# Cross-attention block on one core: softmax sums after the product with V, an x turn behind Q, score groups and loads of the start respread, quotient on GpSimd

## What is computed

```python
x = layer_norm(hidden_states, ln1_w, ln1_b)
q, k, v = x @ q_w + q_b, ctx @ k_w + k_b, ctx @ v_w + v_b        # 16 heads of 32
attn = softmax(where(mask, q @ k.T / sqrt(32), min))             # over 512 keys
hidden = (attn @ v) @ cproj_w + cproj_b + hidden_states
y = layer_norm(hidden, ln2_w, ln2_b)
out = hidden + gelu(y @ fc_w + fc_b) @ proj_w + proj_b
```

## Time and profile before

| | us |
|---|---|
| three runs | 835.57, 841.01, 841.81 (median 841.01) |
| the profiled execution | 834.41, its span 832.6 |
| start, to the first `s2` | 129.8 |
| the 64 steps, from the first `s2` to the first feed-forward matmul | 329.0 |
| from there to the end | 373.9 |
| busy: PE, PEld, DVE, POOL, ACT | 776.1, 526.5, 462.1, 331.6, 284.9 |
| mean granted TensorE clock | 0.975 of 2.4 GHz |

### The profile page before, as it was taken

One profiled execution on the slowest core, in us unless ns is written; L12 is line 12 of the kernel. 1 busy time (PEld: TensorE's weight loads), 2 busy tenths in 40 slices (PEclk: granted clock), 3 DMA queues, 4 the chain that ended last, 5 costly groups with the idle time before them and its releaser, 6 DMA issues.

```text
span 832.6 us, 10079 instructions
## 1 busy us (share of the span) xinstructions
PE 776.1 (93%) x3728; PEld 526.5 (63%) x3728; DVE 462.1 (55%) x967; ACT 284.9 (34%) x495; POOL 331.6 (40%) x202
## 2 busy tenths in 40 slices
PE   7899988898899888988978899999999999999998
PEld 5788753343354334543432588888888888888886
DVE  6865386867766788568785834633323333332222
ACT  4433415766645563556445201121112110111110
POOL 2734402967656676567645535632001110112000
PEclk9999997999999999999996999999999999999999
DMA  8388997666556655435513144304000400011001
GB/s 303 128 285 297 294 258 272 151 154 144 151 141 173 162 148 141 115 78 151 127 42 111 64 140 120 95 1 152 1 0 1 152 1 0 1 62 41 0 1 50
DMA packets 60016, 97.99 MB, mean 118 GB/s; under 512 B 6112, under 2 KB 14564, under 8 KB 59968
## 3 DMA queue, kind: packets, MB, share of 16 engines
q1 hardware_dynamic: 59824, 97.34, 39.4%
q10 hardware_dynamic: 144, 0.02, 0.0%
HBM read 72.03 MB, written 25.18 MB: 117 GB/s over the span
## 4 chain that ended last, share of the span: by engine, by line
PE 72%; DVE 15%; DMA 4%; ACT 3%; issue 3%; SPq 2%; POOL 1%; DVEq 0%; ACTq 0%; POOLq 0%
PE ps L485 18%; PE ps L486 18%; PE ps L487 18%; DVE ps L957 7%; PE ps L582 6%; PE ps L598 4%; PE ps L610 4%; PE ps L567 3%; ACT Pt L778 2%; DVE R L982 1%; DMA qs<-BIG 1%; DVE R L915 1%; DMA R<-in_k_w 1%; DVE BIG L1007 1%; DVE mx L957 1%
## 5 line engine op out<-in xcount | busy, mean ns | idle before, releaser
L957 DVE CUSTOM_DVE_ANT_0 ps<-ps,FU 128x512 f32<-128x512 f32 x256 | 169.1, 723 | 54.9 <-PE ps L567 54.7
L778 ACT ACTIVATE Pt<-ps 128x512 f32<-128x512 f32 x256 | 139.2, 597 | 139.4 <-PE ps L582 136.5
L1110 DVE CAST HR<-R 128x512 fp32r<-128x512 f32 x52 | 24.5, 470 | 183.4 <-ACT R L820 183.4
L1230 POOL TENSOR_TENSOR R<-Pt 128x1024 f32<-128x1024 f32 x30 | 73.0, 2451 | 120.8 <-PE ps L610 77.9
L582 PE MATMUL ps<-BIG 98*128 98x512 f32 x256 | 102.9, 464 | 7.9 <-ACT Pt L778 5.2
L820 ACT ACTIVATE R<-ps,cols 128x512 f32<-128x512 f32 x52 | 35.9, 690 | 205.4 <-PE ps L487 205.4
L582 PEld LDWEIGHTS ps<-BIG 98*128 98x128 f32 x256 | 45.3, 196 | 77.0 <-ACT Pt L778 38.3
L485 PE MATMUL ps<-BIG,HR 128*128 128x512 f32 x192 | 74.9, 390 | 2.7 <-DVE HR L1112 2.7
L485 PE MATMUL ps<-YT,BIG 128*128 128x512 f32 x192 | 75.8, 395 | 0.0
L487 PE MATMUL ps<-YT,BIG 128*128 128x512 f32 x192 | 74.8, 390 | 0.0
L486 PE MATMUL ps<-YT,BIG 128*128 128x512 f32 x192 | 74.8, 390 | 0.0
(11 more groups left out here) (129 smaller groups left out, 1405.5 us busy)
## 6 DMA issues: line engine op xcount, KB each, us to landing
BIG<-qs SPq DMA_DIRECT2D x48, 256.0 KB
BIG<-ks SPq DMA_DIRECT2D x48, 256.0 KB
ks<-BIG SPq DMA_DIRECT2D x32, 256.0 KB, 2.9
qs<-BIG SPq DMA_DIRECT2D x32, 256.0 KB, 6.8
R<-hd SPq DMA_DIRECT2D x28, 256.0 KB, 4.3
R<-in_x SPq DMA_DIRECT2D x16, 256.0 KB, 4.3
hd<-R SPq DMA_DIRECT2D x16, 256.0 KB, 2.2
RW<-in_fc_w SPq DMA_DIRECT2D x16, 256.0 KB, 2.8
```

Source lines behind the costliest of these rows:

```text
L778: eng.activation(Pt[:, r, j % 2, :], bank(PSUM[("s2", i, j)][0]), ACT.Exp, scale=SCALE).then_inc(S["a_ra"], 1)
L957: eng.tensor_tensor_reduce(out=scores, in0=scores, in1=FU[:, s // 4 % 2, :], scale=1.0, scalar=-3.4e38, op0=ALU.add, op1=ALU.max, accum_ou ...
L1230: eng.tensor_tensor(pair_sums(s)[kc // 2][:, 2 * hp:2 * hp + 2, :], Pt[:, (r - 2) % 6, :, :], Pt[:, r, :, :], ALU.add).then_inc(S["g_ac"], 1)
```

## The change

- On TensorE, `sums(s - 1)` stands behind `pv(i - 1)` instead of ahead of it.
- `x_turn(1)`, `x_affine(1)` and `x_high(1)` stand behind all four Q units of batch 0.
- `s1` groups 0 and 1 go to the last two Q units of batch 2, groups 2 to 4 to K of batch 3, group 5 behind the first Q unit of batch 3, ahead of which the first maxima are turned. DVE's maxima follow.
- SP issues the first mask and two leading parts in batch 1. In batch 3 it issues `store_max(0)`, then stack 1, then the eight Q stores, then leading part 2, context 1, stack 2, and only then the projection weight. Before, stacks 1 and 2 stood ahead of K's and Q's stores of batch 3, and context 1 behind the weight.
- The V units of batch 1 start at step 4 and take three steps each; the context splits go to earlier steps.
- `divide_c` goes from DVE to GpSimd, at the head of its step `kc == 3`.
- Layer norm 2 of batch 0 goes to steps 36 to 46. Slab 4 is rounded at step 61 instead of behind the loop, and its low part is made on GpSimd. The last batch's output projection goes one step later.

```diff
@@ plan
-            PARTS[8 + 2 * c] = ([(u, 0)], [(u, 1)], [])
-            PARTS[9 + 2 * c] = ([(u, 2)], [(u, 3)], [])
+            PARTS[4 + 3 * c] = ([(u, 0)], [(u, 1)], [])
+            PARTS[5 + 3 * c] = ([(u, 2)], [], [])
+            PARTS[6 + 3 * c] = ([(u, 3)], [], [])
...
-        SLABS = (50, 56, 57, 60)
+        SLABS = (50, 56, 57, 60, 61)
@@ SP
-                if b == 3:
-                    load_stack(1)
                 for g in range(4):
                     store_qk(b, g, 0)
                 if b == 2:
-                    load_mask(0)
-                    load_lead(0)
-                    load_lead(1)
                     load_stack(0)
...
                 if b == 3:
-                    load_stack(2)
+                    store_max(0)
+                    load_stack(1)
                 for g in range(4):
-                    if b == 3 and g == 2:
-                        store_max(0)
                     store_qk(b, g, 1)
...
+                if b == 1:
+                    load_mask(0)
+                    load_lead(0)
+                    load_lead(1)
             load_lead(2)
+            load_context(1)
+            load_stack(2)
             sp.wait_ge("g_xl", 16)
             eng.dma_start(R2[:, :, :], kp(c_w)).then_inc(S["d_wc"], 16)
@@ TensorE
-                    if b == 3:
-                        s1(g)
+                    if b == 3 and g < 3:
+                        s1(2 + g)
...
-                    if b == 3 and g == 1:
+                    if b == 3 and g == 0:
                         turn_maxima(0)
                     proj_T(b, g, 1)
-                    if b == 0 and g == 1:
-                        x_turn(1)
-                    if b == 3 and g < 2:
-                        s1(4 + g)
+                    if b == 2 and g >= 2:
+                        s1(g - 2)
+                    if b == 3 and g == 0:
+                        s1(5)
+                if b == 0:
+                    x_turn(1)
...
+                if i:
+                    pv(i - 1)
                 if kc == 1 and s:
                     sums(s - 1)
-                if i:
-                    pv(i - 1)
@@ ACT
                     if b == 3 and g == 2:
                         copy_maxima(0)
                     qk_high(b, g, 1)
-                    if b == 0 and g == 1:
-                        x_high(1)
+                if b == 0:
+                    x_high(1)
@@ DVE
-                if kc == 3 and s:
-                    divide_c(s - 1)
...
-                if 30 <= i < 34:
-                    dve.wait_ge(f"d_h{i - 30}", 16)
-                    statistics(HN, 0, 4, i - 30)
...
-                if i in (36, 38, 40, 42):
-                    norm(HN, 0, 4, (i - 36) // 2)
+                if 43 <= i < 47:
+                    norm(HN, 0, 4, i - 43)
@@ GpSimd
+            def divide_c(s):
+                pool.wait_ge("v_t2", s + 1)
+                pool.wait_ge("a_pv", s + 1)
+                if s:
+                    pool.wait_ge("g_al", s)
+                eng.tensor_tensor(R1[:, 3, :], R1[:, 0, :], R1[:, 2, :], ALU.mult).then_inc(S["g_at"], 1)
...
+                if kc == 3 and s:
+                    divide_c(s - 1)
                 if kc % 2:
                     for hp in range(2 if i < 54 else 1):
```

More of the change, by code:

```diff
@@ L422, in _ @@
                     store_max(TURNS[i])
-                if i % 16 == 0 and b < 3:
+                if i in (16, 32):
                     load_context(b + 1)
@@ L457, in _ @@
                         eng.dma_start(ov[4 * (b - 1) + c], R2[:, c, :]).then_inc(S[f"d_o{c}"], 16)
-                if 2 <= i < 6:
-                    c = i - 2
+                if 4 <= i < 8:
+                    c = i - 4
                     sp.wait_ge("v_cp", 12 + c + 1)
@@ L715, in _ @@
                     pj(i - 1)
-                if 2 <= i < 6:
-                    if i < 4:
+                if 3 <= i < 7:
+                    if i < 5:
                         pe.wait_ge("a_pv", NS)
@@ L720, in _ @@
                     else:
-                        pe.wait_ge("v_cp", 12 + i - 3)
-                    cproj(3, i - 2, bank(6 + i % 2)).then_inc(S["p_cp"], 1)
+                        pe.wait_ge("v_cp", 12 + i - 4)
+                    cproj(3, i - 3, bank(6 + i % 2)).then_inc(S["p_cp"], 1)
                 if i < NJ and b + 1 < B and 11 <= f < 15:
@@ L782, in split_out @@
                 ta = R1[:, 3, :]
-                act.wait_ge("v_at", s + 1)
+                act.wait_ge("g_at", s + 1)
                 eng.activation(ta, ta, ACT.Identity, bias=vec[:, 4, g:g + 1]).then_inc(S["a_ab"], 1)
@@ L792, in copy_pv @@
                 if s:
-                    act.wait_ge("v_at", s)
+                    act.wait_ge("g_at", s)
                 else:
@@ L816, in gelu @@
                 elif i in (12, 13):
-                    act.wait_ge("v_at", NS)
+                    act.wait_ge("g_at", NS)
                 else:
@@ L868, in _ @@
                     split_out(s - 2)
-                if b < 3 and i % 16 in (3, 4, 6, 7):
-                    context_high(b + 1, (3, 4, 6, 7).index(i % 16))
+                t = i if b == 0 else i % 16 - 2
+                if b < 3 and 1 <= t < 5:
+                    context_high(b + 1, t - 1)
                 if i in YT_STEPS:
@@ L1007, in split_slab @@
                     eng.tensor_copy(sl[2 * h], RW[:, n, 512 * h:512 * h + 512]).then_inc(S["v_sh"], 1)
-                    if 2 <= f < 5:
+                    if f in (2, 3):
                         dve.wait_ge("v_sh", 2 * f + h + 1)
@@ L1043, in _ @@
                     qk_low(b, g, 0)
-                    if b == 3:
+                    if b == 3 and g < 3:
                         for j in range(4):
-                            maximum(4 * g + j)
+                            maximum(8 + 4 * g + j)
                 if 0 < b < 3:
@@ L1050, in _ @@
                     qk_low(b, g, 1)
-                    if b == 0 and g == 1:
-                        x_affine(1)
-                    if b == 3 and g < 2:
+                    if b == 2 and g >= 2:
                         for j in range(4):
-                            maximum(16 + 4 * g + j)
+                            maximum(4 * (g - 2) + j)
+                    if b == 3 and g == 0:
+                        for j in range(4):
+                            maximum(20 + j)
+                if b == 0:
+                    x_affine(1)
             for i in range(NI):
@@ L1086, in _ @@
                                       ALU.subtract).then_inc(S["v_wc"], 1)
-                if 30 <= i < 34:
-                    dve.wait_ge(f"d_h{i - 30}", 16)
-                    statistics(HN, 0, 4, i - 30)
-                if i == 34:
+                if 36 <= i < 40:
+                    dve.wait_ge(f"d_h{i - 36}", 16)
+                    statistics(HN, 0, 4, i - 36)
+                if i == 40:
                     variances(0, 4)
-                if i in (36, 38, 40, 42):
-                    norm(HN, 0, 4, (i - 36) // 2)
+                if 43 <= i < 47:
+                    norm(HN, 0, 4, i - 43)
                 if i in SLABS:
                     split_slab(SLABS.index(i))
-            split_slab(4)
             split_slab(5)
@@ L1115, in _ @@
                     divide_b(NS - 1)
-                    divide_c(NS - 1)
                 if i >= 1 and f == 0:
@@ L1121, in _ @@
                         eng.tensor_tensor(R2[:, c, :], bank(c), R2[:, c, :], ALU.add).then_inc(S["v_o"], 1)
-                if 2 <= i < 6:
-                    c = i - 2
+                if 3 <= i < 7:
+                    c = i - 3
                     dve.wait_ge("p_cp", c + 1)
@@ L1235, in _ @@
                     out_low(s - 2)
-                if b < 3 and i % 16 in (4, 6, 8):
-                    for k in {4: (0, 1), 6: (2,), 8: (3,)}[i % 16]:
+                t = i if b == 0 else i % 16 - 2
+                if b < 3 and 2 <= t < 5:
+                    for k in ((0, 1), (2,), (3,))[t - 2]:
                         context_low(b + 1, k)
@@ L1245, in _ @@
                     eng.tensor_tensor(R2[:, c, :], R2[:, c, :], cbt[:, :], ALU.add).then_inc(S["g_xc"], 1)
-                if i == 34:
+                if i == 41:
                     root(0, 4)
-                if i in SLABS[:2]:
+                if i in SLABS and SLABS.index(i) not in (2, 3):
                     slab_low(SLABS.index(i))
-            slab_low(5)
             for i in range(NJ):
@@ L1255, in _ @@
                 if i == 0:
+                    divide_c(NS - 1)
                     out_low(NS - 1)
+                    slab_low(5)
                 if 1 <= i < 10:
```

15 lines of the change are left out of this document (5 added, 10 removed).

## The result

| | before | after |
|---|---|---|
| median of 20 runs each, us | 839.13 (835.56 to 844.15) | 843.53 (841.10 to 847.31) |
| ratio after / before | | 1.005, 95% interval 1.0031 to 1.0068 |
| profiled execution, span | 834.41, 832.6 | 841.98, 840.2 |
| mean granted TensorE clock | 0.975 | 0.959 |

The change makes the kernel slower by 0.5%. The forecast was 838 against 841, so 0.4% faster. The loss is small, but its interval leaves out 1. The measured median lies on the wrong side of no change, 7.2 us off (+4.4 instead of -2.8), though inside the range.

A forecast was written before the change was run, and what follows sets the result against it. TensorE bounds the feed-forward part, so only its idle time in start and loop could give; 11.9 - 3.7 - 8.6 - 6.2 + 3.3 + 0.5 = -2.8 us on 834.4 gave 831.6, median forecast 838, range 829 to 851.

The forecast's parts named there:

- The start: Start of the loop: first maxima come earlier, but the projection weight lands at 150.0, delaying step 2's exponentials: +11.9 us.
- M: In the start, the time the first maxima are ready, for which SP waits ahead of stack 1: forecast 119.9, before 122.99.
- the x turn: Second x turn behind batch 0's Q units: the wait moves to Q's third unit, until 40.9; +0.6 us, inside the start's 11.9.
- The promised sign: Profile after: step 2's exponentials wait over 10 us for the weight, ending near 150; under 5 would refute the start's term.
- V spread: Steps 4 to 15: V's units spread at one part per step, 55.8 us becoming 51.9; -3.7 us.
- sums: Sums behind the product with V: the product fills TensorE's wait for the first maximum; -8.6 us, bounds 0 and -11.
- DVE relieved: Steps 40 and 56: norms and quotient no longer stand ahead of maxima on DVE; -6.2 us, bounds 0 and -8.
- Rival 3: Sums' wait only renamed: the next group waits for `divide_a` everywhere, 8.6 us comes back, 847; chance 0.10.
- The quotient on GpSimd: Quotient ahead of GpSimd's pair sums: late only at step 51 (2.5) and step 15 (+0.8); +3.3 us, bounds 0 and +14.
- the sign I had set: Profile after: ACT's L784 waits for GpSimd in step 51 alone; in more than five slices, rival 2 holds.
- rival 2: GpSimd becomes the gate: the quotient reaches ACT 1.3 us late in every slice; +13.4 us, so 854; chance 0.12.
- The joint: Joint ahead of the feed-forward part: slab 4 leaves, but the wait moves to GpSimd; +0.5 us, bounds -3 and +4.

The follow-up runs named there:

- experiment 2: Changed kernel with ACT's four projection-weight copies and DVE's low parts at steps 5 to 8 instead of 1 to 4, loads as changed: 836.3 us, ratio 0.9963 to the kernel before.
- experiment 4: Changed kernel with stack 2 and projection weight loaded in the loop, weight copies and DVE's low parts at steps 7 to 10: 829.02 us, ratio 0.9877 to the kernel before.
- experiment 1: Kernel before with only the sums moved behind the product with V: 833.55 us, ratio 0.9931 to the kernel before.
- experiment 5: Kernel before with only the quotient moved from DVE to GpSimd: 838.23 us, ratio 0.9964 to the kernel before.
- experiment 6: Kernel before with sums behind the product with V and layer norm 2 moved to steps 36 to 46, quotient on DVE: 832.25 us, ratio 0.9899 to the kernel before.
- experiment 3: Changed kernel with the quotient back on DVE at its old place: 844.18 us, ratio 1.0057 to the kernel before.
- experiment 7: Changed kernel with slab 4 split behind the loop again, both halves on DVE: 841.68 us, ratio 1.0011 to the kernel before.
- experiment 10: Changed kernel with GpSimd's third bias add of each batch moved from step 14 to behind step 15's last pair sums: 839.54 us, ratio 1.0006 to the kernel before.
- experiment 11: Experiment 9's kernel plus the third bias add behind the last pair sums: 825.32 us, ratio 0.9815 to the kernel before.
- experiment 12: Experiment 11's kernel with slab 0's low halves behind step 51's last pair sums and SP's reload of that buffer at step 53: 820.98 us, ratio 0.9776 to the kernel before.
- experiment 8: Experiment 4's kernel with slab 4 put back behind the loop: 829.18 us, ratio 0.9857 to the kernel before.
- experiment 9: Experiment 4's kernel with the next batch's context loaded ahead of batch 3's K stores: 827.57 us, ratio 0.986 to the kernel before.

## Why the prediction was wrong

**The start: mechanism right, size 2.7 us short.** The chain from the copy of the maxima to the weight was right to 0.1 us: forecast 30.1, measured 122.18 to 152.37, so 30.2. What was late was M itself, 122.18 instead of 119.9. The waits of 3.0 us in batch 3 were there (0.79, 0.77 and 1.56). Mis-sized were the groups and the x turn. I had taken a group at 0.44 us, but a unit with a group ahead of it and no wait takes 3.41 us from eviction to eviction instead of 2.72, so 0.69; six times the difference is 1.5 us. ACT in the changed kernel:

```profile
102.18 0.69 ACT L761 ACTIVATE BIG<-ps,cols 128x512 fp32r<-128x512 f32 x1 [3.54 <-PE ps L487]
105.59 0.69 ACT L761 ACTIVATE BIG<-ps,cols 128x512 fp32r<-128x512 f32 x1 [2.72 <-PE ps L487]
```

The trace of before shows the same:

```profile
111.04 0.69 ACT L759 ACTIVATE BIG<-ps,cols 128x512 fp32r<-128x512 f32 x1 [7.12 <-PE ps L487]
114.43 0.69 ACT L759 ACTIVATE BIG<-ps,cols 128x512 fp32r<-128x512 f32 x1 [2.70 <-PE ps L487]
```

The turn cost 0.9 us (batch 2's third Q unit is evicted at 94.57 instead of 93.64), not 0.6. Together these are 1.8 of the 2.3 us by which M is late.

The first score came at 126.58, not at 124. Landings followed the order of issue again: the rule of the Trainium skill ("DMA: Bandwidth & Descriptors", section "Queues, rings and completion order") that completion is not first in, first out did not help the weight here. It was issued at 140.06, last but the mask, and landed last but the mask, after 12.3 us. The promised sign, a wait for the weight over 10 us, was seen (11.61), and experiments 2 and 4, which take that wait away, gained 7.2 and 14.5 us. Part of the 2.7 us is the execution compared with: step 4 begins at 146.48 in the trace of before, but at 149.47, 152.64 and 148.08 in those of experiments 1, 5 and 6, whose start is the same; with the changed start it begins at 161.04, and at 161.35, 164.31 and 162.27 in experiments 3, 7 and 10. The middles of the two groups lie 13.0 us apart.

**V spread, sums, DVE relieved: right.** -3.7 against -3.7; steps 18 to 49 and 53 to 58 together -16.2 against -14.2. No wait of L610 for a maximum is left, step 40 takes 4.92 us (forecast 5.3), step 56 5.78. By experiment 6 it is the norms' move that mends step 40, and the quotient's that mends step 56. Rival 3 falls with experiment 1. But the measured 5.6 us (bounds 0 and -11) is below my 8.6, and not because the wait was renamed at its place: the steps without products gave 0.33 instead of 0.55, and steps 12 and 59 became longer by it.

**The x turn: right in the mechanism.** The cost, 0.9 us, is within the bounds. The wait moved to TensorE's third Q unit, until 41.04 (forecast 40.9):

```profile
41.04 0.50 PE L485 MATMUL ps<-BIG,WK 128*128 128x512 f32 x1 [3.26 <-DVE BIG L948]
```

**The quotient on GpSimd: the step that failed.** The sum had it at +3.3: a wait of 0.8 us in step 15 and one of 2.5 in step 51, with nothing behind either.

For "step 15, behind the bias adds, +0.8" the wait was right (0.98 in TensorE) and the price was not: steps 16 and 17 cost +4.8 instead of +0.2. Experiment 4's trace has the same two waits at full clock (10.21 us) and experiment 10's has TensorE's wait for ACT gone (8.99), so that about 1.2 us of the changed kernel's 14.11 are the wait and 3.9 the lower clock. I had priced a drop of the clock behind step 40 but none here. The drop is not this wait's alone: in experiments 6, 11 and 12 it came in these steps without it (0.70 or 0.71, 11.5 to 11.6 us). And the wait comes from terms that I had added as if separate. Experiment 5 shows that the quotient alone does not make it; V spread and the sums' new place take 1.4 and 0.9 us of GpSimd's time. I had checked that the pair sums begin unchanged after the group, and not that the steps behind them begin 0.9 us sooner. It also depends on one bias add ahead of the quotient (experiment 10).

For step 51 I had +2.5 and got +2.4, by luck. In this trace the clock fell in step 50, ahead of ACT's wait of 1.22 us, and TensorE, busy throughout step 51 at the lower clock, never waited for the quotient:

```profile
393.36:398.26 4.90, 4.90 (x20) 1.50 (x16) 4.10 (x10) 2.17 (x4) 4.54 (x4) 0.50 0.00 1
```

In the nine traces with the quotient on GpSimd behind slab 0's low halves steps 50 to 52 took 16.9 to 19.9 us, 19.4 in the middle, so +4.2 on the 15.2 of before. Experiment 12, with the low halves behind, took 14.2.

ACT waited for GpSimd in seven places, where I had named step 51 alone: in five steps of the loop (0.44, 1.66, 0.24, 1.22 and 3.88 us) and twice in and behind the joint (5.36, 5.65). By the sign I had set, more than five, rival 2 holds. By its mechanism, 1.3 us in every slice, it doesn't: nine slices show no wait, and each of the large ones has its own cause in GpSimd's order, a bias add, a slab's low part or a late DVE. Experiment 10, which eased one of them, is 4.0 us faster, and experiment 12, which eased another, 4.3. The nearest of the rivals in effect was this one. Putting the quotient back on DVE is no cure (experiment 3).

**The joint and step 59: underpriced.** Of GpSimd's list in the joint I listed slab 4, quotient and pair sum, 6.5 us together, and still took +0.5 within bounds of -3 and +4; it was +3.5. I had left out the bias add between them (2.28), and again the clock (0.83 in the joint). The term mis-sized is GpSimd's list ahead of the last sums: TensorE waits 3.87 us for it, and with slab 4 put back (experiment 7) 0.83. Step 59 (+2.0) I had not seen at all: SP's load of slab 4 waits until 439.40 for DVE to finish slab 2, whose buffer it takes, and the store of the last maxima stands behind it, on which `s2` of step 60 waits 3.44 us. Step 59 takes 7.17 us in experiment 1, where the sums alone had moved, and 5.23 in experiment 5, where the quotient alone had, so it comes from the sums' new place, which I had taken as free of cost here. How it does so is argued from rows: slab 2's last subtraction on DVE, now beside GpSimd's work, took 1.65 instead of 0.69 us. No run took that away.

**The offset.** I set 831.6 for the profiled execution and added 6.6 us to reach a median. The kernel before's profiled execution lies 4.7 under its median of 20 runs, the changed kernel's 1.5 under its own. So 3.2 us of the 10.4 us miss in the table did not reach the medians, where it is 7.2.

## What to carry to other kernels

A wait that a change adds to the path can have two prices, its length and what TensorE's clock does afterwards; take the second from the stretches of several traces that follow a wait of like length, as a bound of its own, and look whether the clock falls there without the wait too. Two edits that are each free can use up the same slack: shorter steps and more work on the engine that had the room must be summed on that engine's list, place by place. A term that comes out right in the total may still be right by luck; look at which wait made it. And read an in-order queue (SP's too) for what stands behind each new wait: here two loads and the weight's copies later, the context earlier, and one add and one slab's low halves behind the pair sums turned 843.5 us into 821.0.

## What the runs showed of the hardware

- In step 16 TensorE waits for DVE in all fourteen traces (1.1 us; 1.4 in experiment 3). With a second wait behind it, of 1.0 us for ACT, the granted clock over steps 16 and 17 was 0.64 in four traces (the changed kernel, experiments 7, 8 and 9; 14.1 to 14.3 us) and 1.00 in two (experiments 2 and 4; 10.2 us). Without the second wait it was 0.70 or 0.71 in three (experiments 6, 11 and 12; 11.5 to 11.6 us) and 1.00 in five (the kernel before, experiments 1, 3, 5 and 10; 9.0 to 9.3 us). The lower level is 0.50, 1.2 GHz. These are different kernels with one trace each; how often it happens in one kernel was not counted.
- DVE's operations of 128x512 in float32 stretch beside GpSimd: the slab's subtraction took 0.69, 1.65 or 2.73 us in the changed kernel, the quotient on DVE 0.69 to 2.9 us. On GpSimd the quotient took 1.27 to 1.30 us in most slices and up to 2.15 in the changed kernel (2.28 in experiment 10). The Trainium skill ("GPSIMD Engine Reference", section 4.1 "Engine selection") has GpSimd about twice as slow on two inputs; that holds against 0.69, and is reversed where DVE is slowed to 2.75 us or more beside GpSimd.
